# Row statistics of four layer norms taken where the rows are made, row loads cut into 112 and 13 partitions, and the last graph layer ordered by column chunks

## The reference

```python
def _layernorm(x, axis=-1, eps=1e-05):
    m = jnp.mean(x, axis=axis, keepdims=True)
    v = jnp.var(x, axis=axis, keepdims=True)
    return (x - m) / jnp.sqrt(v + eps)

xn = _layernorm(x)
x = x + _L0_gnn_ref(xn, src, dst, ...) + _L0_mix_ref(xn[None], ...)[0]
x = x + _L0_ffn_ref(_layernorm(x)[None], ...)[0]        # 16 experts, top 4, 2 shared
xn = _layernorm(x)
x = x + _L1_gnn_ref(xn, edge_index, ...) + _L1_mix_ref(xn[None], ...)[0]
x = x + _L1_ffn_ref(_layernorm(x)[None], ...)[0]        # 16 experts, top 2, 1 shared
```

```python
for i in range(n_layers):
    x = (x - mean(x, 0)) * rsqrt(var(x, 0) + EPS) * gamma[i] + beta[i]
    agg = segment_sum((x * src_norm)[src], dst, num_segments=N) * dst_norm
    x = relu(agg @ W[i] + b[i])
```

## Time and profile before

| | us |
|---|---|
| median of 3 runs | 2520.39 |
| lowest and highest | 2517.7, 2520.44 |
| the profiled execution | 2525.57 |
| its span in the trace | 2523.8 |
| PE busy | 2206.0 (87%) |
| DVE busy | 997.2 (40%) |
| ACT busy | 513.6 (20%) |
| mean share of the DMA queues q1 and q0 | 13.5% and 8.5% |

### The profile page before, as it was taken

One profiled execution on the slowest core, in us unless ns is written; L12 is line 12 of the kernel. 1 busy time (PEld: TensorE's weight loads), 2 busy tenths in 40 slices (PEclk: granted clock), 3 DMA queues, 4 the chain that ended last, 5 costly groups with the idle time before them and its releaser, 6 DMA issues. The chain is left out here.

```text
span 2523.8 us, 26899 instructions
## 1 busy us (share of the span) xinstructions
PE 2206.0 (87%) x7344; PEld 1261.0 (50%) x7345; DVE 997.2 (40%) x2712; ACT 513.6 (20%) x900; POOL 286.1 (11%) x317
## 2 busy tenths in 40 slices
PE   4998979999978988783998989979899898799996
PEld 2444434444444455441543468844488644445553
DVE  6967873202035422121133455412355203634443
ACT  1112221111103022221210154211244112201111
POOL 0200000000000045452210000000000100012332
PEclk9999999999998999997999989989999999899998
DMA  3003000000004166665001000020000103048784
GB/s 117 1 0 110 1 1 17 1 17 0 1 0 133 58 145 152 156 149 142 17 0 54 4 1 1 1 91 0 0 1 1 38 0 115 21 152 263 198 252 114
DMA packets 77159, 159.34 MB, mean 63 GB/s; under 512 B 9027, under 2 KB 20334, under 8 KB 77010
## 3 DMA queue, kind: packets, MB, share of 16 engines
q1 hardware_dynamic: 59410, 115.62, 13.5%
q0 software_dynamic: 17664, 42.64, 8.5%
HBM read 122.06 MB, written 38.74 MB: 64 GB/s over the span
## 5 line engine op out<-in xcount | busy, mean ns | idle before, releaser
L1785 PE MATMUL bank<-arena 125*125 125x257 f32 x1600 | 355.7, 383 | 4.7 <-DVE arena L1704 4.7
L1785 PEld LDWEIGHTS bank<-arena 125*125 125x125 f32 x1600 | 302.2, 189 | 60.4 <-DVE arena L1704 6.3
L2023 PE MATMUL bank<-arena 128*128 x832 | 251.6, 453 | 31.1 <-issue 16.1
L893 PE MATMUL bank<-arena 125*128 125x500 f32 (+1 forms) x720 | 252.6, 512 | 2.3 <-ACT arena L918 2.3
L2023 PEld LDWEIGHTS bank<-arena 128*128 128x128 f32 x832 | 157.7, 195 | 147.2 <-issue 87.3
L1600 PE MATMUL bank<-arena 128*125 128x512 f32 x480 | 211.2, 600 | 8.9 <-DMA arena<-in_L_gnn_W 8.9
L448 PE MATMUL bank<-arena 128*125 128x512 f32 x480 | 213.9, 595 | 2.2 <-PEq L280 1.1
L2041 PE MATMUL bank<-arena 128*128 x360 | 177.1, 621 | 33.2 <-ACT arena L2069 24.6
L893 PEld LDWEIGHTS bank<-arena 125*128 125x128 f32 x720 | 135.7, 189 | 120.5 <-issue 110.6
L2115 DVE TENSOR_TENSOR arena<-bank,arena 128x384 f32<-128x384 f32 (+1 forms) x104 | 51.6, 497 | 311.7 <-PE bank L2023 280.9
L1763 ACT ACTIVATE arena<-arena 125x625 f32<-125x625 f32 x160 | 134.5, 902 | 102.4 <-DVE arena L1704 102.2
(11 more groups left out here) (324 smaller groups left out, 2224.2 us busy)
## 6 DMA issues: line engine op xcount, KB each, us to landing
arena<-in_L_ffn_expert_w SPq DMA_DIRECT2D x16, 1536.0 KB
arena<-in_L_ffn_re_w SPq DMA_DIRECT2D x32, 512.0 KB
arena<-in_L_ffn_expert_w SPq DMA_DIRECT2D x16, 768.0 KB
arena<-in_L_mix_Wqkv SPq DMA_DIRECT2D x6, 1024.0 KB, 8.3
arena<-in_L_ffn_expert_b SPq DMA_DIRECT2D x16, 384.0 KB
token_rows<-arena SPq DMA_DIRECT2D x2, 2500.0 KB
token_sums<-arena SPq DMA_DIRECT2D x20, 250.0 KB
arena<-in_L_gnn_W SPq DMA_DIRECT2D x1, 4096.0 KB, 13.0
```

The costliest lines, as they stand in the source:

```text
L893: last = pe.matmul(st.bank[4 + n % 4][:, 0:cn], h[:, s, f * P:(f + 1) * P], st.counts[:, s, c0:c0 + cn], start=(s == 0), stop=(s == NT - 1))
L1785: return pe.matmul(st.bank[n % OUTS][0:TS, 0:ONCOL], prob[:, u % 2, s, j * TS:(j + 1) * TS], st.slots[:, head + 1, s, :], start=(s == 0), ...
L2023: last = pe.matmul(st.bank[UP[b][h]][:, 0:WP], xt[b][:, k, :], rt.ring[:, bass.ds(r, 1), k * W + h * WP:k * W + (h + 1) * WP].rearrange("p ...
```

## The change

What it does:

1. `st.row_stats` and `st.row_means` are kept for the whole program (80 words, `DYN` moves from 12534 to 12614). A new `row_moments` takes statistics and aggregations of given tiles. It is called in `stage_setup` and `stage_routed` after each half of the load, in the last graph layer after each pair of additions, and in `stage_linear` after each addition. `stage_layernorm` begins with the square root.
2. `load_tiles` loads tiles `t0:t1` by two DMAs, of partitions 0 to 111 and 112 to 124. `x` in setup and the sums after the routed experts come in two halves of five tiles, so four DMAs in place of one. In setup they are issued ahead of the parameters.
3. The attention's weight loads are issued in `stage_setup` and at the end of `stage_routed`, behind the row loads.
4. In the last graph layer the 12 products go by chunk (`fc_last`, `c` outermost). PE turns tiles 0 to 3 back after product 5, 4 to 7 after 9, 8 and 9 after 11; DVE adds them and takes their moments after 6, 7, 10 and 11.
5. The cast to 16 bits and the self loops go to the first graph layer, one tile after each of the products 0 to 9; `st.counts` keeps no self loops. The stage at L931 falls away.
6. `levels` start at -1, so an expert with `count` tokens gets floor(count / 128) + 1 tiles, and `routed_steps` allows for it.

```diff
+EVEN = 112
+HALVES = [(0, 5), (5, 10)]
...
-    return (top * NODES + NE * (slots - 1)) // slots
+    return (top * NODES + NE * slots) // slots
...
+def load_tiles(sp, to, rows, t0, t1, loaded):
+    rows = rows.rearrange("(t p) d -> p t d", p=TS)
+    sp.dma_start(to[0:EVEN, t0:t1, :], rows[0:EVEN, t0:t1, :]).then_inc(loaded, 16)
+    sp.dma_start(to[EVEN:TS, t0:t1, :], rows[EVEN:TS, t0:t1, :]).then_inc(loaded, 16)
+
+def row_moments(dve, st, tiles, summed):
+    for t in tiles:
+        dve.bn_stats(st.row_stats[:, t, :], st.res3[:, t, :]).then_inc(summed, 1)
+    for t in tiles:
+        dve.wait_ge(summed, t + 1)
+        dve.bn_aggr(st.row_means[:, t, :], st.row_stats[:, t, :])
...
@@ stage_setup, sync
+            for h, (t0, t1) in enumerate(HALVES):
+                load_tiles(sp, st.res3, x, t0, t1, x_loaded[h])
             for i, v in enumerate(graph_par):
                 sp.dma_start(par_rows[i * LK:(i + 1) * LK, :],
                              v.rearrange("l (k p) -> (l k) p", p=P)).then_inc(par_loaded, 16)
-            sp.dma_start(st.res3, x.rearrange("(t p) d -> p t d", p=TS)).then_inc(x_loaded, 16)
-            sp.wait_ge(x_loaded, 16)
+            load(sp)
+            sp.wait_ge(x_loaded[0], 32)
+            sp.wait_ge(x_loaded[1], 32)
@@ stage_setup, vector, behind L252
+            for h, tiles in enumerate(HALVES):
+                dve.wait_ge(x_loaded[h], 32)
+                row_moments(dve, st, range(*tiles), summed)
@@ stage_layernorm
-            for t in range(NT):
-                dve.bn_stats(stats[:, t, :], st.res3[:, t, :]).then_inc(stats_ready, 1)
-            for t in range(NT):
-                dve.wait_ge(stats_ready, t + 1)
-                dve.bn_aggr(moments[:, t, :], stats[:, t, :]).then_inc(moments_ready, 1)
...
-            act.wait_ge(moments_ready, NT)
-            act.activation(std, moments[:, :, 1], ACT.Sqrt, bias=st.eps[0:TS, :]).then_inc(std_ready, 1)
+            act.activation(std, st.row_means[:, :, 1], ACT.Sqrt, bias=st.eps[0:TS, :]).then_inc(std_ready, 1)
@@ stage_graph
+    fc_last = [(f, c) for c in range(3) for f in range(KT)]
+    TURN_AFTER = {5: (range(0, 4), 4), 9: (range(4, 8), 8), 11: (range(8, NT), 12)}
+    ADD_AFTER = {6: range(0, 2), 7: range(2, 4), 10: range(4, 6), 11: range(6, NT)}
...
+                    if i == 0 and n < NT:
+                        own = slice(n * TS, (n + 1) * TS)
+                        dve.tensor_copy(st.counts16[:, n, :], st.counts[:, n, :]).then_inc(cast, 1)
+                        dve.wait_ge(cast, n + 1)
+                        dve.tensor_tensor(st.counts16[:, n, own], st.counts[:, n, own], st.ident[0:TS, 0:TS], ALU.add)
+                    if last and n in ADD_AFTER:
+                        tiles = ADD_AFTER[n]
+                        for t in range(tiles.start, tiles.stop, 2):
+                            for u in (t, t + 1):
+                                dve.wait_ge(final_turned, u + 1)
+                                dve.tensor_tensor(st.res3[:, u, :], st.res3[:, u, :], st.bank[u % 4][0:TS, :],
+                                                  ALU.add).then_inc(added, 1)
+                            dve.wait_ge(added, t + 2)
+                            row_moments(dve, st, (t, t + 1), summed)
...
+            def turn_back(tiles, placed):
+                pe.wait_ge(out_placed, LAYERS * 12 + placed)
+                for t in tiles:
+                    if t >= 4:
+                        pe.wait_ge(added, t - 3)
+                    for k in range(KT):
+                        last = pe.transpose(st.bank[t % 4][0:TS, k * P:(k + 1) * P],
+                                            X[:, k, t * TS:(t + 1) * TS], st.ident)
+                    last.then_inc(final_turned, 1)
...
-            for s in range(NT):
-                part = st.counts[:, s, s * TS:(s + 1) * TS]
-                dve.tensor_tensor(part, part, st.ident[0:TS, 0:TS], ALU.add).then_inc(looped, 1)
-            dve.wait_ge(looped, NT)
-            dve.tensor_copy(st.counts16, st.counts)
@@ stage_front, iotas
-            for out, by in ((levels, SLOTS), (step_no, 1), (even, 2)):
+            for out, by, at in ((levels, SLOTS, -1), (step_no, 1, 0), (even, 2, 0)):
@@ stage_linear, vector, behind the addition of tile t
+                dve.wait_ge(y_added, t + 1)
+                row_moments(dve, st, (t,), summed)
@@ stage_routed, sync
-                sp.dma_start(st.res3, sums[1:NODES + 1, :].rearrange("(t p) d -> p t d", p=TS)).then_inc(sums_read, 16)
+                for h, (t0, t1) in enumerate(HALVES):
+                    load_tiles(sp, st.res3, sums[1:NODES + 1, :], t0, t1, sums_read[h])
+                load(sp)
+                sp.wait_ge(sums_read[0], 32)
+                sp.wait_ge(sums_read[1], 32)
@@ stage_routed, vector, at the end
+            if out is None:
+                for h, tiles in enumerate(HALVES):
+                    dve.wait_ge(sums_read[h], 32)
+                    row_moments(dve, st, range(*tiles), summed)
```

More of the change, by code:

```diff
@@ L269, in _, with stage_layernorm @@
             pe.transpose(st.bank[4][:, 0:3 * LK], par_rows, st.ident[0:3 * LK, 0:3 * LK]).then_inc(par_turned, 1)
-def stage_layernorm(nc, st, ar, kept=None, load=None):
-    stats = ar.take(NT * 6, TS).rearrange("p (t s) -> p t s", s=6)
-    moments = ar.take(NT * 2, TS).rearrange("p (t s) -> p t s", s=2)
+def stage_layernorm(nc, st, ar, kept=None):
     std, rstd, shift = (ar.take(NT, TS) for _ in range(3))
@@ L846, in _ @@
                     dve.wait_ge(row_ready, 6)
-                for n, (f, c) in enumerate(fc):
+                last = i + 1 == LAYERS
+                for n, (f, c) in enumerate(fc_last if last else fc):
                     c0, cn = CHUNKS[c]
@@ L895, in _ @@
                     last.then_inc(agg_ready, 1)
+                    if i + 1 == LAYERS and n in TURN_AFTER:
+                        turn_back(*TURN_AFTER[n])
                 pe.wait_ge(agg_scaled, (i + 1) * 12)
                 pe.wait_ge(out_placed, (i + 2) * 12)
-            for t in range(NT):
-                if t >= 4:
-                    pe.wait_ge(added, t - 3)
-                for k in range(KT):
-                    last = pe.transpose(st.bank[t % 4][0:TS, k * P:(k + 1) * P],
-                                        X[:, k, t * TS:(t + 1) * TS], st.ident)
-                last.then_inc(final_turned, 1)
         @block.scalar
```

70 lines of the change are left out of this document (31 added, 39 removed).

## The result

| | before | changed kernel |
|---|---|---|
| median of the timed runs, us | 2520.41 (2517.7 to 2530.55, 4 runs) | 2486.31 (2484.04 to 2497.71, 4 runs) |
| profiled execution, us | 2525.57 | 2487.18 |
| its span, us | 2523.8 | 2485.1 |
| mean granted clock of its span | 0.956 | 0.962 |

The ratio is 0.9866 with an interval of [0.9847, 0.9885]: 34.1 us by the medians, 38.4 by the two profiled executions. The forecast was 43.3 less, 2477.1. The time lies inside the stated range, near its upper end, and 9.2 us above the sum, so some of the 43.3 didn't come. It is also 1.3 us from the 2487.6 of rival 1, whose cause didn't occur; that closeness is luck. In a second set of runs on one chip, the changed kernel took 2486.43 beside 2524.19 of before, 37.8 us less.

What follows compares the result with a forecast made beforehand. The prediction took TensorE, busy 87% of the span, as the bound, with gains only in its waits at four hand-overs. 9.4 + 13.6 + 15.7 + 4.6 = 43.3 us off 2520.4 gave 2477.1, range 2470 to 2488.

Steps and rivals of the forecast that it cites:

- rival 1: At both split row loads, the 13 partitions go by one engine: 32.8 us saved in all, time 2487.6; chance 8%.
- What bounds the kernel: Whole kernel: TensorE is busy 87% of the span, so an edit pays only where TensorE stands still.
- First hand-over: Setup to first norm: split, earlier load of `x` and moments before the norm start the square root 9.4 us earlier.
- Second: Graph to second norm: a stage and the statistics removed, 32 transposes costing 4.1 us; square root 13.6 us earlier.
- rival 5: Last graph layer: DVE can't place its pairs between scalings and TensorE waits 1 to 5 us, time 2478 to 2482; 7%.
- Third: Routed experts to third norm: split load, fullest engine 6.6 us at 25 GB/s; square root 15.7 us earlier.
- rivals 1 and 2: Rival 1, and rival 2: row loads still go by five engines, 25.0 us saved in all, time 2495.4, chance 4%.
- My bounds for the unknown: Row loads by engine count: five engines save 4.0 (first) and 2.8 (third); 13 partitions by one, 7.9 and 6.7.
- Fourth: Linear to fourth norm: nine tiles' moments hide in a wait for TensorE; square root 4.6 us earlier.
- rival 3: Norms one, three and four: table loads hide behind the barrier's wait, 3 x 1.28 us more saved, time 2473.3; 5%.
- The levels that start at -1: Routed experts: the new tile formula adds no tile, 48 and 28 as before; cost at nothing, at most 0.5 us.
- rival 4: TensorE's clock: about 1 us gained each at norms two and four, or turned slower, time near 2526; chance 3%.

Runs made afterwards that it cites:

- e1: The changed kernel with the three small parameter loads issued ahead of the `x` row loads: 2481.89 us, one execution.
- e12: The changed kernel run once more with nothing altered, on the same chip as e9 and e10: median 2486.43 us, ratio to before 0.9847.
- e8: The changed kernel with its graph part undone (order, transposes, additions, moments, cast and self loops as before): median 2502.41 us, ratio to before 0.9935.
- e3: The changed kernel without the 13-partition parts of the load after the routed experts, those rows keeping old values: 2488.06 us, one execution.
- e6: The changed kernel loading only the 13-partition parts after the routed experts, the 112 others keeping old rows: 2472.55 us, one execution.
- e5: The changed kernel loading 120 partitions a half after the routed experts, the last five keeping old rows: 2488.92 us, one execution.
- e4: The changed kernel with each half loaded in one transfer of 125 partitions, at both row loads: 2523.48 us, one execution.
- e2: The changed kernel with the attention's weight loads issued in the norm's stage again, after the row loads: 2483.13 us, one execution.
- e9: The changed kernel with each half after the routed experts loaded as one transfer of 128 partitions: median 2480.67 us, ratio to before 0.9825.
- e7: The changed kernel with parameters first, three dummy square roots, and 120 partitions plus a separate five-partition load after the routed experts: median 2481.56 us, ratio 0.9852.
- e10: The changed kernel with e9's 128-partition load, parameters ahead of `x` and three dummy square roots: median 2474.47 us, ratio to before 0.9796.
- e11: e5 with each partition's rows read from other places in DRAM, the destination kept: 2482.72 us, one execution.

## Why the prediction was right, and where it wasn't

The places and the chain that ends last at each of them were right. The sum was too high by one wrong rate, that of an engine which loads 112 or 13 partitions. It counted twice: in the load at the third hand-over, and at the first through the parameters, which stood behind `x`.

1. **What bounds the kernel.** Confirmed: TensorE's busy time is unchanged, and all four terms are steps between marks of the same chain.
2. **First hand-over, 9.4 forecast, 7.1 measured.** The step that failed is "the parameters land behind `x`, near 12.5, and DVE copies them at 15.77 in any case". They landed at 18.19, right behind `x` (17.62), since `x` didn't run at the rate that it was costed with, and TensorE waited 4.78 us for them. With the parameters ahead (e1) the square root is at 24.41, against 24.6 in the sum, by two small errors that cancel: the copy is 0.36 later than 15.77, and the moments take 6.7 us where the sum had 7.1. By the second execution of the changed kernel (e12) this term is 6.1.
3. **Second, 13.6 forecast, 14.4 measured.** The 32 transposes cost 3.5 where I counted 4.1; the rest was right to 0.2 us, and e8 gives 14.35 for it. The pairs fit between the scalings: rival 5 didn't happen. Cast and self loops at nothing hold: TensorE's idle time ahead of the three layers' products is the same 2.3 us in both (the line of before, then that of the changed kernel), and e8, which has them back in a stage of their own, starts its last layer 0.4 us later, not earlier.

```profile
L893 PE MATMUL bank<-arena 125*128 125x500 f32 x480 | 203.5, 582 | 2.3 <-ACT arena L918 2.3
```

```profile
L937 PE MATMUL bank<-arena 125*128 125x500 f32 x480 | 203.2, 582 | 2.3 <-ACT arena L957 2.3
```

4. **Third, 15.7 forecast, 10.6 measured: the term that was mis-sized.** The counts of engines were right. A share of 1.04 alone shows that for 112 partitions only, since behind 13 the weights keep the other engines busy. The semaphore events show both: a load's count rises by 16 single steps for 112 partitions (e3), and by one step at the issue and then 13 for 13 partitions (e6), 15 for 120 (e5) and 5 for 125 (e4), where five engines is also what the share says. So rivals 1 and 2 are out. The step that failed is "6.6 us at 25 GB/s" for the fullest of 16 engines. I took the rate of an engine from loads of 125 and 128 partitions, and used it for divisions that no row showed. The third load moved 152 to 294 GB/s where the sum had 16 x 25. The shortfall of 5.1 us was divided by experiment: the 13 partitions 4.05 (e3), the weights behind them 0.9 (e2; the two overlap), and a load of 128 at 388 GB/s takes all of it back (e9, 14.27 after the issue where the sum had 14.1). My bounds for the unknown went by how many engines there are, and not by how fast they are beside each other.
5. **Fourth, 4.6 forecast, 4.6 measured**, the exposed table load included; e7 and e10 take just that 1.28 away.
6. **The table loads** stand in the open at norms 1, 3 and 4 and at no other: rival 3 didn't happen by itself, and was there to be had with three dummy instructions.
7. **The levels that start at -1** add no tile: the group of the first layer's tiles counts 48 again and that of the second 28, as in the earlier trace rows.

```profile
L2111 ACT ACTIVATE arena<-arena 128x256 f32<-128x256 f32 x48 | 20.1, 418 | 61.0 <-DVE arena L2149 61.0
...
L2108 ACT ACTIVATE arena<-arena 128x384 f32<-128x384 f32 x28 | 17.2, 616 | 112.6 <-DVE arena L2162 112.6
```

8. **The clock.** The slow turn of rival 4 didn't come: the granted clock was 1.00 in every window of the last layer from 690 to 738. Its small gain came at one of the two places. At norm 2 the clock was 0.50 in 740 to 744 and the transposes took 6.80 us (6.44 before); at norm 4 it was 0.77 in 2066 to 2068 and they took 5.93 (7.06 before). Behind norm 4 more than that was lost: the gate products began after a wait of 4.81 us (2.93 before) and took 11.48 (8.57 before).

```profile
2102.75 7.06 PE L316 MATMUL bank<-arena 125*128 125x125 f32 x40 [9.18 <-DVE arena L306]
...
2112.74 8.57 PE L1175 MATMUL bank<-arena 128*16 128x500 f32 x24 [2.93 <-DMA arena<-in_L_ffn_gate_w]
```

```profile
2063.91 5.93 PE L334 MATMUL bank<-arena 125*128 125x125 f32 x40 [4.62 <-DVE arena L324]
...
2074.65 11.48 PE L1202 MATMUL bank<-arena 128*16 128x500 f32 x24 [4.81 <-DMA arena<-in_L_ffn_gate_w]
```

TensorE's next products start 23.55 us after the fourth square root, 19.89 before, so 3.7 of the 38.84 were gone there. From those products to the end the changed kernel then took 3.5 less than before (399.04 for 402.56), and nothing here says why; the 38.84 of the mark and the 38.7 of the span agree by luck. The loss isn't a fixed price of the change: in e12 the step is 21.57.
9. **From terms to the median.** The terms measured, 36.6, and 2.3 us between the hand-overs are 38.8 at the fourth mark. The profiled execution of before lay 5.2 us above its median and that of the changed kernel 0.9, so the medians show 4.3 less. On the second chip the difference of the medians was 37.8. The sum was made against one execution and taken off a median of three; the scatter of medians over single executions is a few microseconds, and this part of the miss can't be put down to the kernel.

What stays open: the 2.3 us between the hand-overs are 1.0 between the second norm and the third load's issue, and 1.3 between the third norm and the last addition of the linear stage. In e12, the same kernel, both stretches are longer than before (by 0.7 and 0.4), so the 2.3 are no more than the difference of two executions. The 3.5 us regained after the gate products weren't followed up. Nor did I test by itself that blocks are contiguous. The model comes near four sizes, and e9 and e11 exclude the byte count and the source, but it doesn't give e4, and a fifth size was not run.

## What to carry to other kernels

Before you cost a split load, ask two things: how many engines it gets, and what rate they reach together into those partitions. A DMA share near 1 shows only that engines are busy; the GB/s beside it shows whether they move anything. If tiles have a few rows less than 128, load all 128 partitions and let the rest fall on unused ones: here it was 5 us faster than 112 and 13, at more bytes. The source must then have a few rows behind the last (`token_sums` has 1408 for 1250 tokens). Put small loads that an engine will soon wait for ahead of the large one in the queue, and when statistics move out of a norm, move its table load with them.

## What the hardware showed that I had not expected

- A busy engine is not a fast one: at shares of 1.02 to 1.06 the 16 engines moved 388 GB/s (128 partitions), 296 (112), 215 (120, 15 engines and the weights) and 105 (13 engines and the weights).
- Two transfers that are each at full rate alone hurt each other: 125 partitions by five engines at 84 ns a row, 155 to 164 for nearly all packets beside the weights (e4).
- SP's issue of a load gets long when the engines' queues are full. Three weight loads took SP 5.75 us behind the split rows, 9.52 in e7, 17.80 in e4, 1.50 with idle queues (e2). In the changed kernel none of it was on a path that set an end. In e4 one parameter load took SP 8.03 us, but the last parameter was issued at 18.82 and landed at 32.78, right behind `x` (32.17), so its place in the queue held it up and not the issue.
- The gate products after norm 4 ran at one clock level in some executions and began at the other in others. In the changed kernel that wait was 4.81 us, the granted clock was 0.50 (the 1.2 GHz level) while they began, and they took 11.5 us; in e7 the wait was 2.95, the clock stayed 1.00 and they took 8.6, as in the kernel before (2.93 and 8.57). The wait alone doesn't order them: 3.27 in e1 and 4.51 in e10 both went with some 10.3. Windows of the changed kernel and then of e7:

```profile
2074.00:2076.00 2.00, 1.35 (x2) 0.28 (x3) 0.00 (x0) 0.00 (x0) 0.00 (x0) 0.50 0.40 34
```

```profile
2070.00:2072.00 2.00, 1.75 (x5) 0.46 (x6) 0.00 (x0) 0.00 (x0) 0.00 (x0) 1.00 0.35 40
```

  The load of `gate_w` landed 1.9 us after its issue in e7 and 3.6 in the changed kernel, 3.2 in its second profile. What makes it so is open; part of what differs between executions may be this.
